# A two-layer recurrent kernel on one core: moved products, narrower TensorE tiles, norms as rows

## The reference, cut to what matters

```python
x = L0_attn_x                                   # (16, 256, 128)
xn = _layernorm(x)
s = _L0_attn_ref(xn, Wqkv, Wout, bout)          # layer 1 of the kernel's text: linear attention
#   q, k = elu(q)+1, elu(k)+1 ; kv = k.T v ; ks = k.sum ; out = (q kv) / (q ks + eps) ; out @ Wout + bout
g = _silu(_L0_ffn_ref(xn, ...))                 # softmax attention (16 heads of 8, causal), top-2 of 8 experts
x = x + s * g
xn = _layernorm(x)
s = _L1_attn_ref(xn, Wq, Wk, Wv, Wg, bg, Wo, ...)
#   q, k = l2_normalize per head ; alpha = sigmoid(xn Wg + bg) ; log_a = log(alpha)
#   per chunk of 64 tokens: la_cum = cumsum(log_a), decay from its mean over d,
#   attn_intra = (q k.T) * decay ; o_intra = attn_intra v ; kv_chunk = (k * decay_to_end).T v
#   state S passed from chunk to chunk ; o = o_intra + (q exp(la_cum)) S ; out = o @ Wo, LN, gelu FFN
g = _silu(_L1_ffn_ref(xn, ...))                 # top-1 of 8 experts
x = x + s * g
```

## Time and profile before

| | us |
|---|---|
| median of 3 runs | 2235.43 (2231.66 to 2240.91) |
| the profiled execution | 2234.39 |
| its span in the trace | 2232.6 |
| TensorE busy | 1934.6 (87%) |
| VectorE busy | 1362.9 (61%) |
| ScalarE busy | 1096.1 (49%) |
| GpSimd busy | 214.6 (10%) |

### The profile page before, as it was taken

How to read it: one execution, slowest core, us unless ns; L and a number is a source line. 1 busy time by engine, 2 the same in 40 slices (tenths; PEclk the granted TensorE clock), 3 DMA queues, 4 the chain that set the end, 5 groups by cost and what they waited for, 6 DMA issues and landing times.

```text
span 2232.6 us, 50773 instructions
## 1 busy us (share of the span) xinstructions
PE 1934.6 (87%) x17956; PEld 1381.8 (62%) x17972; DVE 1362.9 (61%) x3678; ACT 1096.1 (49%) x2434; POOL 214.6 (10%) x235
## 2 busy tenths in 40 slices
PE   6999999998999999959888988898988899898652
PEld 4666666666666666636667566765766676666552
DVE  6666666666666666637665765577666566755312
ACT  3444444443555445425665465555555554555332
POOL 0000000000000000030011001101111110010022
PEclk9999999999999999969999999999999999999887
DMA  3222222222122211230221112110211111111374
GB/s 127 79 87 87 87 87 92 91 86 64 59 68 68 67 49 53 75 116 23 63 67 47 56 56 66 52 30 24 67 46 58 58 53 41 37 46 42 124 233 119
DMA packets 97041, 159.05 MB, mean 71 GB/s; under 512 B 14279, under 2 KB 65607, under 8 KB 93640
## 3 DMA queue, kind: packets, MB, share of 16 engines
q1 hardware_dynamic: 87720, 134.93, 18.7%
q0 software_dynamic: 9248, 23.17, 3.4%
HBM read 96.35 MB, written 61.69 MB: 71 GB/s over the span
## 4 chain that ended last, share of the span: by engine, by line
PE 59%; DVE 20%; ACT 7%; issue 7%; SPq 3%; DMA 2%; POOL 1%; another core or an unknown queue 1%; DVEq 0%; ACTq 0%; POOLq 0%
PE psum L1032 5%; PE psum L870 5%; PE psum L937 4%; PE psum L830 4%; PE psum L764 3%; PE psum L1012 3%; PE psum L987 3%; PE psum L1142 3%; PE psum L952 2%; PE psum L1090 2%; PE psum L959 2%; PE psum L786 2%; PE psum L904 2%; PE psum L1041 2%; PE psum L877 2%
## 5 line engine op out<-in xcount | busy, mean ns | idle before, releaser
L1349 ACT ACTIVATE pts<-psum 128x512 f32<-128x512 f32 x192 | 99.1, 603 | 201.1 <-PE psum L904 201.1
L1803 DVE TENSOR_REDUCE mneg<-psum 128x2 f32<-128x512 f32 (+1 forms) x192 | 119.1, 683 | 46.8 <-PE psum L885 25.1
L671 POOL DMA_INDIRECT rows<-h,recA x64 | 61.5, 961 | 894.7 <-DVE recA L1585 767.3
L786 PE MATMUL psum<-txT,wt 128*128 128x128 f32 x864 | 118.9, 281 | 32.1 <-ACT txT L1241 32.0
L786 PEld LDWEIGHTS psum<-txT,wt 128*128 128x128 f32 x864 | 106.7, 194 | 43.9 <-ACT txT L1241 38.4
L870 PE MATMUL psum<-wa,xT_s 128*128 128x512 f32 x256 | 118.0, 603 | 2.6 <-DVE mneg L1803 2.6
L1032 PE MATMUL psum<-xT_s,wa 128*128 128x256 f32 x512 | 116.6, 381 | 0.0
L695 POOL DMA_INDIRECT rows<-xn,recC x32 | 31.5, 983 | 861.5 <-DVE recC L2007 741.3
L1550 DVE TENSOR_TENSOR tg<-tg,psum 128x256 f32<-128x256 f32 x84 | 35.2, 419 | 113.6 <-ACT tg L1230 109.2
L1032 PEld LDWEIGHTS psum<-xT_s,wa 128*128 128x128 f32 x512 | 95.8, 192 | 12.9 <-issue 1.0
L795 PE MATMUL psum<-wt,tg 128*128 128x128 f32 x528 | 79.2, 280 | 14.6 <-DVE tg L1552 13.8
(11 more groups left out here) (272 smaller groups left out, 4862.7 us busy)
## 6 DMA issues: line engine op xcount, KB each, us to landing
wt<-in_wB SPq DMA_DIRECT2D x84, 384.0 KB, 2.9
outs<-pbd SPq DMA_DIRECT2D x16, 1024.0 KB, 7.2
wt<-in_wD SPq DMA_DIRECT2D x24, 578.0 KB, 3.5
wa<-in_wD SPq DMA_DIRECT2D x15, 578.0 KB, 3.6
tx<-rows SPq DMA_DIRECT2D x132, 64.0 KB, 2.9
outs<-ty SPq DMA_DIRECT2D x132, 64.0 KB, 1.6
rows<-pbd SPq DMA_DIRECT2D x64, 128.0 KB, 1.7
rows<-pbd SPq DMA_DIRECT2D x8, 1024.0 KB, 3.9
```

Source lines behind the costliest of these rows:

```text
L786: last = mm(bank(f"th{j}")[:, c * P:(c + 1) * P], view[s][:, c * P:(c + 1) * P], txT[:, s, :], start=True, stop=True)
L1349: af(pT[:, n, :], bank(f"e{n}"), ACT.Exp, scale=float(HD) ** -0.5).then_inc(*frees(f"e{n}"))
L1803: ins = v.tensor_reduce(mneg[:, int(n >= 4), col:col + hs], sc, AX.X, ALU.max, negate=True)
```

## The change

Layer 1: the linear output (transposes of `o_tok`, product with `wout0`) of an element is no longer at the end of its own body but in the middle of the next one: `outputs_turned(0)` after `scores(1)`, `outputs_turned(1)` after `tile_step(2)`, `linear_output` between the two `numerators`; on DVE it stands between `divided(0)` and `divided(1)`. In GP, which has no A, all three stand behind the gate, and on DVE ahead of `rows_given`. `oT` moves from the keys' place to that of `e_q`. `kv` and `numerators` become products of 64 columns or rows in halves and quarters of the array, without the unused blocks; the masks of the second and third part of the scores shrink from 512 to 256 columns.

Layer 2: the key product `lk` moves from the end of a body to the beginning of the next, the decays (ACT) and their means (DVE) the other way. The squared norms of queries and keys become 32 rows per group by four narrow products each (bank nq), are raised once for both in one 128 x 512 tile, the keys' are transposed (rkT), the queries' spread again by `headrow` (rb). The keys in token form are transposes of `kT` (tk), and stay in the bank until kd is made. d, te and la are made in 64 x 64 quarters, with the two chunks of a token tile stored with rows exchanged for the upper half of the heads (`chunk_rows`). The bias products of z stand ahead of the wait, each on its own 32 rows, for which `ones3` and `bg3` are loaded four times (12 small copies in place of 3).

```diff
@@ uses_in_order: stage A, stage C
+        over("oT00", "oT01")
-        names += [f"kv{j}" for j in range(4)]
+        names += [f"kv{j}" for j in range(2)]
...
+        over("oT10", "oT11")
...
+        over("s0")
...
-        names += ["oT00", "oT01", "pn0", "pd0", "oT10", "oT11"]
+        names += ["pn0", "pd0"]
...
-        names += [f"nq{j}" for j in range(4)]
-        names += [f"tk{t}{c}" for t in range(NT) for c in range(2)]
-        tile_step(0)
-        tile_step(1)
         names += [f"d{t}{c}" for t in range(NT) for c in range(2)]
         names += [f"te{t}{c}" for t in range(NT) for c in range(2)]
+        names += [f"lk{j}" for j in range(4)]
+        tile_step(0)
+        names += ["nq"]
+        tile_step(1)
         names += [f"tv{t}{c}" for t in range(NT) for c in range(2)]
+        names += ["rkT"] + [f"rb{j}" for j in range(4)]
+        names += [f"tk{t}{c}" for t in range(NT) for c in range(2)]
@@ SyncE
             for i in range(3):
-                sp.dma_start(bg3[i:i + 1, :], kd_b16(i)).then_inc(sem("bg3_ready"), 16)
+                for g in range(4):
+                    sp.dma_start(bg3[32 * g + i:32 * g + i + 1, :], kd_b16(i)).then_inc(sem("bg3_ready"), 16)
@@ TensorE, z
+                for g, (t, c) in enumerate(places):
                     pe.wait_ge(*emptied(f"z{t}{c}"))
+                    mm(bank(f"z{t}{c}"), ones3[32 * g:32 * g + 3, :], bg3[32 * g:32 * g + 3, c * 512:(c + 1) * 512], start=True, stop=False)
+                pe.wait_ge(*read_out("zT"))
+                for t in range(NT):
+                    mm(bank(f"z{t}0"), xT[:, 1, t * P:(t + 1) * P], lqkvg[:, 3 * INNER:3 * INNER + 512], start=False, stop=True).then_inc(*fills(f"z{t}0"))
+                    pe.sem_inc(sem("tiles_open"), 1)
+                    for ch in range(2):
+                        place = chunk_rows(1, ch)
+                        last = mm(bank(f"z{t}1")[place, :], xT[:, 1, t * P + ch * CH:t * P + (ch + 1) * CH], lqkvg[:, 3 * INNER + 512:4 * INNER], start=False, stop=True)
@@ TensorE, attention0
-                for j in range(4):
-                    pe.wait_ge(*emptied(f"kv{j}"))
-                    for a in range(2):
-                        pr = 2 * j + a
+                for hh in range(2):
+                    pe.wait_ge(*emptied(f"kv{hh}"))
+                    for a in range(4):
                         for t in range(NT):
-                            last = mm(bank(f"kv{j}")[:, a * N:a * N + 2 * V0], k_tok[:, t, pr * P:(pr + 1) * P],
-                                      v_tok[:, t, 2 * pr:2 * pr + 2, :], start=(t == 0), stop=(t == NT - 1))
+                            for c in range(2):
+                                hd = 2 * (4 * hh + a) + c
+                                last = mm(bank(f"kv{hh}")[c * DH:(c + 1) * DH, a * V0:(a + 1) * V0], k_tok[:, t, hd * DH:(hd + 1) * DH],
+                                          v_tok[:, t, hd, :], start=(t == 0), stop=(t == NT - 1))
@@ TensorE, numerators
+                        for a in range(4):
+                            for ch in range(2):
+                                tokens = slice(t * P + ch * CH, t * P + (ch + 1) * CH)
+                                for c in range(2):
+                                    rows = slice(c * DH, (c + 1) * DH)
+                                    last = mm(bank(f"num{t}{2 * hh + c}")[ch * CH:(ch + 1) * CH, a * V0:(a + 1) * V0], qt[rows, 4 * hh + a, tokens],
+                                              kvb[rows, 4 * hh + a, :], start=True, stop=True)
@@ TensorE, attention1
+                quads = [(hh, ch) for hh in range(2) for ch in range(2)]
+                for t in range(NT):
+                    for hh in range(2):
+                        pe.wait_ge(*emptied(f"d{t}{hh}"))
+                        mm(bank(f"d{t}{hh}"), identb[:, :], dmask[:, :, :], start=True, stop=False)
+                    pe.sem_inc(sem("tiles_open"), 1)
+                    for hh, ch in quads:
+                        rows = chunk_rows(hh, ch)          # the 64 rows of chunk ch ^ hh
+                        last = mm(bank(f"d{t}{hh}")[ch * CH:(ch + 1) * CH, :], strict[rows, rows], at3[rows, t, 8 * hh:8 * hh + 8, :], start=False, stop=True)
...
+                    for hh, ch in quads:
+                        rows = chunk_rows(hh, ch)
+                        last = mm(bank(f"te{t}{hh}")[ch * CH:(ch + 1) * CH, :], strict[rows, rows], a_tok[rows, t, hh * 512:(hh + 1) * 512], start=True, stop=True)
...
+                products("lk", INNER)
+                tile_step(0)
+                pe.wait_ge(*given("sk_done", 4))
+                for j in range(4):
+                    pe.wait_ge(*read_out(f"lk{j}"))
...
+                for i, squares in enumerate((sqT, sqK)):
+                    for a in range(2):
+                        for j in range(4):
+                            last = mm(bank("nq")[32 * j:32 * j + 32, i * N:(i + 1) * N], headsum[:, a, :], squares[:, 2 * j + a, :], start=(a == 0), stop=(a == 1))
...
+                for a in range(2):
+                    for j in range(4):
+                        rows = slice(32 * j, 32 * j + 32)
+                        last = mm(bank(f"rb{j}")[:, a * N:(a + 1) * N], headrow[rows, a, :], rqk[rows, 0, :], start=True, stop=True)
...
+                        for a in range(4):
+                            last = tr(bank(f"tk{t}{c}")[:, a * P:(a + 1) * P], kT[:, 4 * c + a, t * P:(t + 1) * P])
@@ VectorE, attention0 and attention1
+                divided(0)
+                linear_output()
                 divided(1)
...
-                for j in range(4):
-                    dve.wait_ge(*filled(f"nq{j}"))
-                    v.tensor_scalar(sqT[:, 2 * j:2 * j + 2, :], bank(f"nq{j}").rearrange("p (a n) -> p a n", a=2), 1e-24, None, ALU.max).then_inc(*frees(f"nq{j}"))
...
-                        v.tensor_copy(k_tok[:, t, c * 512:(c + 1) * 512], bank(f"tk{t}{c}")).then_inc(*frees(f"tk{t}{c}"))
-                v.tensor_reduce(small[:, 96:128], ks_row.rearrange("p (h d) -> p h d", d=DH), AX.X, ALU.add).then_inc(*signals("dve_chain"))
```

More of the change, by code:

```diff
@@ L139, in uses_in_order @@
     else:
-        over("hT")
-        over("gate")
+        over("hT", "gate", "oT00", "oT01", "oT10", "oT11", "s0")
         for u in range(tiles_in(stages)[0] + 2):
@@ L861, in h2_turned, with outputs_turned, linear_output @@
                 last.then_inc(*fills("hT"))
+            def outputs_turned(t):
+                if "G" not in now["stages"]:
+                    return
+                pe.wait_ge(*given("o_ready", t - 1))
+                for c in range(2):
+                    pe.wait_ge(*emptied(f"oT{t}{c}"))
+                    for a in range(4):
+                        last = tr(bank(f"oT{t}{c}")[:, a * P:(a + 1) * P], o_tok[:, t, (4 * c + a) * P:(4 * c + a + 1) * P])
+                    last.then_inc(*fills(f"oT{t}{c}"))
+            def linear_output():
+                if "G" not in now["stages"]:
+                    return
+                pe.wait_ge(*emptied("s0"))
+                pe.wait_ge(*read_out("oT11"))
+                for t in range(NT):
+                    for pr in range(NP):
+                        last = mm(bank("s0")[:, t * P:(t + 1) * P], oT[:, pr, t * P:(t + 1) * P], wout0[:, pr, :], start=(pr == 0), stop=(pr == NP - 1))
+                last.then_inc(*fills("s0"))
             def attention0():
@@ L876, in scores @@
                         pe.wait_ge(*emptied(use))
-                        mm(bank(use), identb[:, :], diag_mask if part == 0 else row_mask, start=True, stop=False)
+                        if part == 0:
+                            mm(bank(use), identb[:, :], diag_mask, start=True, stop=False)
+                        else:
+                            mm(bank(use).rearrange("p (h n) -> p h n", h=2)[:, :, P:N], identb[:, :], diag_mask_2, start=True, stop=False)
                     heads = GR if part == 0 else 2
@@ L884, in scores @@
                             else:
-                                last = mm(bank(use)[:, a * N:(a + 1) * N], qr[p0:p0 + HD, 2 * (part - 1) + a, P:N], kr[p0:p0 + HD, :], start=False, stop=(a == heads - 1))
+                                for kt in range(NT):
+                                    last = mm(bank(use)[:, a * N + kt * P:a * N + (kt + 1) * P], qr[p0:p0 + HD, 2 * (part - 1) + a, P:N], kr[p0:p0 + HD, kt * P:(kt + 1) * P],
+                                              start=False, stop=(a == heads - 1 and kt == NT - 1))
                             if a == heads - 1:
@@ L1022, in attention0, with products @@
                 tile_step(7)
-            def first_qk(name, off):
-                if "P" not in now["stages"]:
-                    return
+            def products(name, off):
                 for j in range(4):
@@ L1057, in attention1 @@
[L1057 to L1060 removed]
+                        for j in range(4):
```

(28 more changed lines are left out.)

349 lines of the change are left out of this document (180 added, 169 removed).

## The result

The changed kernel took 2265.21 us, the kernel before 2238.14 on the same chip (four runs each): ratio 1.0124, 95% interval 1.0097 to 1.0151. It is slower by 1.2%, where 111 us less were forecast. The profiled execution took 2266.75 (span 2265.0).

A forecast was written before the change was run, and what follows sets the result against it. The prediction took TensorE, busy 87% of the span, as the bound. C bodies 73, AHG 16, tiles 28 and first body 6 made 123 us less, start and GP 12 more: 2235.4 - 111 = 2124 us, range 2095 to 2155, chance 0.50.

The forecast's parts named there:

- prices of the products: TensorE: four narrow 512-column products side by side 0.85 to 1.07 us; kv 2.05, numerators 2.2, z 3.8.
- new waits ahead of nq: Layer 2, start of a C body: nq waits for ACT's reads of d, te and lk, TensorE 1.6 us idle.
- Rival 3: Layer 2: narrow products sharing a bank run in turns; 2229 us with three turns, 2281 with four; chance 0.15.
- C body: 2.6 + 1.6 + 0.7: Layer 2: earlier last state, shorter z and body's end save 4.9 us per C body, rounded to 4.7.
- the last state at 35.5 us: C body: DVE's last state stands 35.5 us after the body's start, before at 38.1; 2.6 us less.
- other two terms (1.6 + 0.7): C body: z 1.6 us shorter, 5.4 to 3.8, and the body's end 0.7 us shorter.
- Rival 2: Waits longer than walked, or the clock falls in tile and C bodies too; 2155 to 2200 us; chance 0.18.
- only 0.7 less: C body's end: lk's 3.4 us leave, but ACT's queue and a 1.2 us feed-forward wait leave 0.7 us saved.
- 2 us less: Layer 1, AHG bodies: each 2 us shorter, 5.0 at full clock; bounds 0 and 5.
- 4 less: Layer 1, bodies with tiles: each 4 us shorter, clock at 1.00; bounds 0.5 and 6.
- GP: Between the layers: linear output at low clock and table on DVE cost 6 us more; bounds 2 and 12.
- start: Kernel start: 12 bias copies instead of 3 cost 6 us more, bounds 3 and 8; first AH body 6 less.

The follow-up runs named there:

- pad320: The kernel before with 320 empty semaphore increments on TensorE in one place of layer 2's C body, ahead of the wo1 products; 3010 us.
- fit: la16_lkend with the decay products d 128 wide again and eleven waits that later ones cover left out; 2233.98 us, 0.9994 of the kernel before.
- fit_shift: fit with 60 empty instructions at the very start of TensorE's program, outside every loop; 2215.35 us, 0.9917 of the kernel before.
- nar_q_shift: fit_shift with layer 1 that of narrow_l1 and the decay products d in quarters again; 2181.24 us, 0.9767 of the kernel before.
- la16_lkend: The changed kernel with la as 16 full products again and the key products lk back at the body's end; 2220.53 us, 0.9919 of the kernel before.
- narrow_l1: The kernel before with only layer 1's narrow kv, numerators and masks, linear output left at its body's end; 2230.00 us, ratio 0.9963.
- l1only: The kernel before with all of the change's layer 1, moved linear output included, and layer 2 as before; 2229.92 us, ratio 0.9998.
- nar_lkend_unrolled: The changed kernel with the linear output left where it was, lk at the body's end and layer 2's two loops written out; 2191.28 us, 0.9812 of before.
- la_wide: The changed kernel with la as 32 products of 128 rows by 64 columns in place of 64 quarter products; 2308.29 us, 1.0348 of the kernel before.

## Why the prediction was wrong

**The prices of the products were right at full clock.** te 0.96 us per group (forecast 0.95), kv 2.02 (2.05), numerators 1.18 (1.1), nq 1.87 (1.7), z 4.1 (3.8), the new waits ahead of nq 1.8 (1.6) and ahead of the feed-forward 1.2 (1.2). Rival 3 falls: te's quarters share a bank from two groups of rows and four take 0.96 us together, and d does as well at full clock (1.09 with the overlap). The three or four turns that it counts with show in no run. The 0.4 us that d and z were each given for changes between full and narrow products was my estimate, and no row shows it; z took 4.1 us, where four banks at 0.86 make 3.4.

**The step that failed** is the first term of "C body: 2.6 + 1.6 + 0.7": the last state at 35.5 us after the start of the body. It priced a narrow product by its time in the array alone and gave its instructions no cost. The change puts 345 more instructions into a loop of 1515; it no longer stays loaded and is fetched in each pass (9 packets). In the body shown above the output product behind the last state (L1207) starts 45.3 us after the end of the body before it (1324.93 to 1370.19), and nothing releases it: TensorE came late, not VectorE. The 9.8 us over 35.5 are about what three things add up to: the standstill at the start 2.9, d at half clock 2.3 (5.6 for 3.3), and the standstills in the groups of small products 4.7. The rest of this body took 30.7 us where it had taken 33.4, so the other two terms (1.6 + 0.7) held there. Over the loop: forecast -4.7 per body, measured +1.2 (525.75 - 517.50, over 7). No rival had it. Rival 2 came nearest by its sign in the profile (0.95 in C, where it asked for less than that), with another cause and too small a price. The cause is shown by pad320, by fit against fit_shift, and by the start gap that unrolling removes. The half clock isn't the fetching's alone (nar_q_shift: 0.50 for 3 us in a loop without a packet).

**Second, "only 0.7 less" at the body's end.** ScalarE's queue was walked once, with tiles, where L1239 waits 1.7 us; in bodies without tiles it waits up to 3.8, and 43.0 in all where L1163 had waited 22.4. Moving lk back to the end gave 25 us (la16_lkend), but mostly by the waits ahead of nq and of the feed-forward's first product, both of which the walk had priced (1.6 and 1.2 us); the 39.0 us ahead of the second product stayed.

**Third, AHG "2 us less" and tiles "4 less":** measured +0.5 and +0.1. I expected the fall of the clock in AHG once; it came twice per body, and in two of six tile bodies in full too (65.8 and 66.5 us, clock 0.90, against 62.1 at 1.00). The AHG bodies miss the bounds 0 and 5, the tile bodies 0.5 and 6, since a wait was priced at its length, without the half clock behind it. The 2 us of AHG are the walk's 5 less 3 for one fall of the clock; no run shows these 3 as a time of their own. Read in windows of 0.5 us, the clock stood at 0.50 for some 6 of the 7.4 us of the earlier trace rows, which costs about 3 us by my estimate (half of 6), and for 10.5 us in narrow_l1. l1only, with the same layer 1, took 13.5 us less for its six tile bodies than the changed kernel (370.1 and 383.7); why the clock fell less often there isn't shown.

**GP** +10.8 for +6, inside its bounds; **start** +1.3 with the first body for +6 and -6. VectorE lost 125 us of work, not 176.

Of the gap of 141 us to the forecast (2265.2 against 2124), runs give: about 21 the jump back (unrolling; its fetching remains), 25 the key products' place, 16 the moved output. nar_lkend_unrolled undoes these three together and took 2191.28, some 70 us less than the changed kernel. The other half of the gap stays open in its parts; the 74 us that unrolled code still waits for issue and the clock of the remaining bodies (0.94 to 0.97) lie in it, and I can't price them alone.

## What to carry to other kernels

Dividing products into quarters bought array time with instructions here (layer 2's seven bodies: 40 us less of TensorE work, 345 more instructions in the loop with tiles, 8 us longer). Before pricing such an edit, count the loop's instructions and look at the packets of the instruction queue within one pass: none, as in the loops of the kernel before, means that there is something to lose; the changed kernel had 36 in four passes and 45 in five. A gap put down to issue at the start of a loop body was the sign of that loss (2.9 to 3.5 us a pass); shortening the loop, or shifting where it begins, gave the gap back here (19 us in fit_shift). A wait is also dearer than its length where half clock follows it (in narrow_l1 10.5 us at 0.50 behind waits of 1.32 and 1.52 us): look at the granted clock behind it before pricing a saving.

## What the runs showed of the hardware

- A TensorE loop of 1664 instructions stayed loaded (la_wide, no packet in five passes), one of 1661 (la16_lkend, 36 packets in four) or 1639 (fit, 25 in four) at another place didn't. Fetched anew, a loop took up to 9 packets of 16 KB per pass, and 2.9 to 3.5 us of standstill at the jump in the changed kernel's loop with tiles, at most 1.1 in its loop without.
- Sixty empty instructions at the program's start made it 19 us faster, and the 25 packets in four passes went to none (fit, fit_shift).
- A bare semaphore increment on TensorE takes 0.135 us in a loop that is fetched (691.4 us over 16 bodies of 320, pad320) and 0.11 at the program's start (60 move the first product from 6.98 to 13.59 us, fit and fit_shift).
- With 128x128 fp32 weights, 64 records of 64 columns take 7.4 us in a row (la_wide), 0.115 us each; those of 128 columns take 0.120 to 0.124. Half the columns saved next to nothing.
- Four 64x64 fp32 products of 512 columns, two groups of rows writing one bank, take 0.96 us together at full clock (te).
